# Routed layers of a decoder: indirect scatters into slots replaced by a list made on PE and indirect loads

## What is computed

```python
# L0f (top 2, GELU, hidden 512) and L2f (top 2, RMS norm, gated SiLU, hidden 448)
logits = h @ W_router                       # 2048 x 8
v, idx = top_k(logits, 2); w = softmax(v)
out = sum_k w[:, k] * expert[idx[:, k]](h)  # two products with W1, W2
# L1f (top 1, layer norm, GELU, hidden 512, at most 256 tokens of an expert)
p = softmax(logits); e = argmax(p)
out = p[e] * expert[e](h)  where the token's rank in its expert is below 256, else 0
```

## Time and profile before

| | us |
|---|---|
| median of 3 runs | 1659.69 (1654.34 to 1673.64) |
| the profiled execution | 1662.46 |
| its span | 1660.70 |
| PE busy in the span | 1188.7 (72%) |
| DVE busy | 1058.3 (64%) |
| ACT busy | 626.4 (38%) |
| POOL busy | 616.4 (37%) |

### The profile page before, as it was taken

One profiled execution on the slowest core, in us unless ns is written; L12 is line 12 of the kernel. 1 busy time (PEld: TensorE's weight loads), 2 busy tenths in 40 slices (PEclk: granted clock), 3 DMA queues, 4 the chain that ended last, 5 costly groups with the idle time before them and its releaser, 6 DMA issues. The chain is left out here.

```text
span 1660.7 us, 35597 instructions
## 1 busy us (share of the span) xinstructions
PE 1188.7 (72%) x14040; PEld 901.0 (54%) x14040; DVE 1058.3 (64%) x2869; ACT 626.4 (38%) x1475; POOL 616.4 (37%) x694
## 2 busy tenths in 40 slices
PE   6983508858999869664677854099938885776878
PEld 5652408746888646553344643088825551563556
DVE  4888711147999748835678498234379937856772
ACT  2551104314777736222454321022214433543433
POOL 4347353432333235443233025623343333424320
PEclk9995559978999879777687565599969866876879
DMA  8900035550000078031000100345410000000000
GB/s 267 153 3 2 12 100 162 185 168 23 3 3 3 3 100 110 6 91 55 1 1 1 27 1 9 105 132 182 150 51 2 1 1 1 2 2 1 1 1 26
DMA packets 72010, 89.13 MB, mean 54 GB/s; under 512 B 5823, under 2 KB 59138, under 8 KB 71200
## 3 DMA queue, kind: packets, MB, share of 16 engines
q1 hardware_dynamic: 65824, 76.89, 19.5%
q0 software_dynamic: 6016, 9.93, 1.7%
HBM read 56.55 MB, written 32.69 MB: 54 GB/s over the span
## 5 line engine op out<-in xcount | busy, mean ns | idle before, releaser
L766 POOL TENSOR_TENSOR arena<-arena,small 128x1024 f32<-128x1024 f32 x80 | 154.7, 1939 | 112.2 <-ACT arena L649 70.1
L380 POOL TENSOR_SCALAR var_eps<-moments 128x1 f32<-128x1 f32 (+1 forms) x136 | 35.7, 262 | 367.1 <-DVE moments L373 367.1
L697 ACT ACTIVATE arena<-arena 128x1024 f32<-128x1024 f32 x80 | 84.6, 1058 | 136.8 <-DVE arena L844 136.7
L564 PE MATMUL ps<-arena,q 64*64 64x512 f32 x640 | 103.3, 719 | 39.1 <-issue 17.6
L574 PEld LDWEIGHTS ps<-small,arena 128*128 128x128 f32 x640 | 82.7, 159 | 65.0 <-ACT arena L697 32.8
L722 ACT COPY arena<-ps 128x512 f32<-128x512 f32 x160 | 87.3, 588 | 67.3 <-PE ps L574 66.5
L574 PE MATMUL ps<-small,arena 128*128 128x128 f32 x640 | 100.4, 307 | 10.8 <-ACT arena L697 10.0
L1608 PEld LDWEIGHTS ps<-expert_ring,arena 128*128 128x128 f32 (+1 forms) x864 | 104.5, 192 | 2.9
L1608 PE MATMUL ps<-expert_ring,arena 128*128 128x128 f32 (+1 forms) x864 | 104.7, 275 | 0.0
L586 PE MATMUL ps<-vx,arena 128*64 128x18 f32 x2560 | 99.6, 222 | 3.1 <-issue 2.8
L586 PEld LDWEIGHTS ps<-vx,arena 128*64 128x64 f32 x2560 | 91.2, 151 | 18.4 <-issue 14.8
(11 more groups left out here) (360 smaller groups left out, 2925.6 us busy)
## 6 DMA issues: line engine op xcount, KB each, us to landing
expert_ring<-L2f_in SPq DMA_DIRECT2D x23, 704.0 KB, 4.2
expert_ring<-L0f_in SPq DMA_DIRECT2D x23, 578.0 KB
slots_L0f<-blank SPq DMA_DIRECT2D x1, 8385.0 KB, 56.7
slots_L2f<-blank SPq DMA_DIRECT2D x1, 8385.0 KB, 56.6
small<-small_in SPq DMA_DIRECT2D x1, 4231.5 KB, 19.2
expert_ring<-L1f_in SPq DMA_DIRECT2D x8, 512.0 KB
arena<-slots_L0f SPq DMA_DIRECT2D x23, 129.0 KB, 3.2
arena<-slots_L2f SPq DMA_DIRECT2D x23, 129.0 KB, 3.5
```

Of the source, the lines that this page charges most:

```text
L564: last = pe.matmul(c.ps[part(b), m], c.q[part(m), at:at + S], kx(t)[part(m), b * 512:(b + 1) * 512], start=True, stop=True)
L697: act.activation(buf(k), buf(k), ACT.Exp, scale=exp_scale).then_inc(s.probs_ready, 1)
L766: g.tensor_tensor(kx(t).rearrange("p (b h k) -> p b h k", b=2, k=S), bcast(of_tile, 2, HEADS // 2), bcast(bcast(c.w("head_of_row"), 2, S), ...
```

## The change

Rows no longer pass through a table of slots. SP stores the tokens plainly in DRAM, four DMAs as quarters become ready. For each quarter DVE (`mark_cells`) and POOL (`mark_columns`) form one-hot rows from the slot numbers: a slot is split into a column (its low seven bits) and a start, one operand holds the token's number + 1 at the start's place, the other a 1 at the column's. PE multiplies them and adds up over all tiles (`invert_slots`), which gives the number of the token in each slot. For top 2 a further product (`find_rows`) picks the rows of the 23 blocks; `list_rows` on DVE makes of them the tokens to fetch and the places to return to, and marks empty slots. POOL fetches each block with two indirect loads of 128 rows (`fetch`), four blocks ahead, in the same list as the returns. The blank tables, the row copies on ACT, the row loads of SP and the cast of `home` go; the blank table of L1f's results stays. Of the diff, cut:

```diff
@@ routed_experts: SP
-        sp.wait_ge(c.scattered, c.scattered_before[n] + 16 * NT * top)
-        for j in range(3):
-            load_rows(j, first[j])
-        for j in range(BLOCKS):
-            if j + 3 < BLOCKS:
-                load_rows(j + 3, row_of_block(j + 3))
-            if j >= SLOTS:
-                load_routed(j)
+        by_tile = tokens_dram.rearrange("(p t) d -> p t d", t=NT)
+        for q in range(QUARTERS):
+            if twice:
+                sp.wait_ge(r.ready, HT * (q + 1))
+            sp.dma_start(by_tile[:, own(q)], src[:, own(q)]).then_inc(s.stored, 16)
...
+        for j in range(SLOTS, BLOCKS):
+            load_routed(j)
@@ PE
+        def invert_slots(q):
+            pe.wait_ge(s.cells_a, HT * top * (q + 1))
+            pe.wait_ge(s.cells_b, HT * top * (q + 1))
+            for i in range(HT * top):
+                first, final = q == 0 and i == 0, q == QUARTERS - 1 and i == HT * top - 1
+                if capped:
+                    last = pe.matmul(found_ps, cells_b(q)[:, i], cells_a(q)[:, i], start=first, stop=final)
+                else:
+                    last = pe.matmul(inverse_ps, cells_a(q)[:, i], cells_b(q)[:, i], start=first, stop=final)
+            last.then_inc(s.inv_ps, 1)
+        def find_rows():
+            pe.wait_ge(s.inv_ready, 1)
+            pe.wait_ge(s.mapped, 11)
+            pe.matmul(found_ps, inverse, chosen, start=True, stop=True).then_inc(s.found_ps, 1)
...
             if q > 0:
                 rank(q - 1)
+            if q > 1:
+                invert_slots(q - 2)
...
+        invert_slots(QUARTERS - 2)
+        invert_slots(QUARTERS - 1)
+        if not capped:
+            find_rows()
@@ ACT
-            if not twice:
-                for k in range(top):
-                    act.copy(rows(k)[:, own(q), 0:D], c.h[:, own(q)]).then_inc(s.rows, 1)
-            if twice and top == 2:
-                act.wait_ge(r.ready, HT * (q + 1))
-                act.copy(rows(1)[:, own(q), 0:D], rows(0)[:, own(q), 0:D]).then_inc(s.rows, 1)
+        if not capped:
+            act.wait_ge(s.inv_ps, QUARTERS)
+            act.copy(inverse, inverse_ps).then_inc(s.inv_ready, 1)
@@ POOL
+        def mark_columns(q):
+            g.wait_ge(s.column, 3 * q + 2)
+            if q >= 2:
+                g.wait_ge(s.inv_ps, q - 1)
+            for i, t in enumerate(tiles_of(q)):
+                for k in range(top):
+                    g.tensor_scalar(cells_b(q)[:, i * top + k], c.w("lane"), T[:, t, 15, k:k + 1], None, ALU.is_equal)\
+                        .then_inc(s.cells_b, 1)
+        def fetch(j):
+            if j >= 5:
+                g.wait_ge(s.xT_ps, j - 4)
+            for k in range(PER):
+                at = c.token_of[:, PER * j + k:PER * j + k + 1]
+                g.indirect_dma_start(xs(j)[:, k], None, tokens_dram[:, :],
+                                     bass.IndirectOffsetOnAxis(ap=at, axis=0),
+                                     bounds_check=NT * P - 1, oob_is_err=False).then_inc(c.fetched[j % 5], 16)
         for q in range(QUARTERS):
-            g.wait_ge(s.slot_index, q + 1)
...
+            mark_columns(q)
+        g.wait_ge(s.stored, 16 * QUARTERS)
+        g.wait_ge(s.listed, 5)
+        for j in range(4):
+            fetch(j)
+        if capped:
+            g.wait_ge(c.blanked[n], 16)
         for j in range(BLOCKS):
+            if j + 4 < BLOCKS:
+                fetch(j + 4)
             g.wait_ge(s.y_ready, j + 1)
-            g.wait_ge(s.home, j + 1)
@@ DVE
-            v.tensor_scalar(c.slot[:, own(q), 0:top], T[:, own(q), 10, 0:top], float(NOWHERE) if capped else 0.0,
-                            None, ALU.add).then_inc(s.slot_index, 1)
+            v.tensor_scalar(slot, T[:, own(q), 10, 0:top], float(NOWHERE) if capped else 0.0, None, ALU.add)\
+                .then_inc(s.placed, 1)
+            v.wait_ge(s.placed, q + 1)
+            v.tensor_scalar(column, slot, P - 1, None, ALU.bitwise_and).then_inc(s.column, 1)
+            v.wait_ge(s.column, 3 * q + 1)
+            v.tensor_copy(T[:, own(q), 15, 0:top], column).then_inc(s.column, 1)
+            v.tensor_tensor(T[:, own(q), 15, 4:4 + top], slot, column, ALU.subtract).then_inc(s.column, 1)
+        def mark_cells(q):
+            v.wait_ge(s.column, 3 * q + 3)
...
+            for i, t in enumerate(tiles_of(q)):
+                for k in range(top):
+                    v.tensor_scalar(cells_a(q)[:, i * top + k], c.w("lane_start")[:, 0:CELLS], T[:, t, 15, 4 + k:5 + k],
+                                    numbers[:, k, t:t + 1], ALU.is_equal, ALU.mult).then_inc(s.cells_a, 1)
+        def list_rows():
...
+            v.tensor_scalar(number, found_ps, -1.0, 0.0, ALU.add, ALU.max).then_inc(s.listed, 1)
...
         place(0)
+        mark_cells(0)
...
         if not capped:
             map_blocks()
+        list_rows()
         weigh()
@@ take_slots: DVE
-            v.tensor_copy(c.home[:, PER * j:PER * j + PER], xs(j)[:, :, D]).then_inc(s.home, 1)
```

More of the change, by code:

```diff
@@ L292, in room, with blank_homes @@
         return self.arena[:, k * 1024:(k + n) * 1024]
[L294 to L297 removed]
+    def blank_homes(self, sp, n):
+        sp.dma_start(self.home_dram[n].rearrange("(p t) d -> p t d", t=NT), bcast(self.blank[:], 1, NT))\
             .then_inc(self.blanked[n], 16)
[L299 to L301 removed]
     def load_expert(self, sp, layer, e):
@@ L492, in attention @@
     block = c.block
[L493 to L496, removed]
     @block.tensor
@@ L1672, in _ @@
         for k in range(top):
-            g.tensor_scalar(rows(k)[:, :, D], c.w("token_home"), float(k * NT * P), None, ALU.add)\
+            g.tensor_scalar(numbers[:, k], c.w("token_number"), float(k * NT * P), None, ALU.add)\
                 .then_inc(s.constants, 1)
@@ L1766, in map_blocks @@
             count, upto_e = scratch(224, E), scratch(232, E)
-            of_block, region, before, inside, offset = (scratch(640 + 32 * k, TOP2_BLOCKS) for k in range(5))
+            of_block, region, before, inside, column = (scratch(640 + 32 * k, TOP2_BLOCKS) for k in range(5))
             by_j = lambda a: a.rearrange("p (j e) -> p j e", e=E)
@@ L1789, in map_blocks @@
             v.wait_ge(s.mapped, 9)
-            v.scalar_tensor_tensor(out=offset, in0=inside, scalar=float(PER * P), in1=region, op0=ALU.mult,
+            v.scalar_tensor_tensor(out=column, in0=inside, scalar=float(PER), in1=region, op0=ALU.mult,
                                    op1=ALU.add).then_inc(s.mapped, 1)
             v.wait_ge(s.mapped, 10)
-            v.tensor_scalar(c.block_row[:], offset[0:1], float(E * NT * P), None, ALU.min).then_inc(s.block_row, 1)
+            for k in range(PER):
+                last = v.tensor_scalar(chosen.rearrange("p (j k) -> p j k", k=PER)[:, :, k], column, float(k),
+                                       c.w("own_lane"), ALU.add, ALU.is_equal)
+            last.then_inc(s.mapped, 1)
         def weigh():
@@ L1864, in _ @@
         place(1)
+        mark_cells(1)
         for q in range(2, QUARTERS):
@@ L1867, in _ @@
             place(q)
+            mark_cells(q)
         if not capped:
             map_blocks()
+        list_rows()
         weigh()
@@ L1930, in _ @@
     def _(sp):
-        c.blank_slots(sp, "L1f")
+        c.blank_homes(sp, "L1f")
     @block.tensor
@@ L2774 @@
 STAGES = {
-    "L0a": lambda c: attention(c, "L0a", mode="bias", q_scale=HD ** -0.5, bias=True, out_bias=True,
-                               blanks="L0f"),
+    "L0a": lambda c: attention(c, "L0a", mode="bias", q_scale=HD ** -0.5, bias=True, out_bias=True),
     "L0x": channel_attention,
@@ L2779 @@
     "L1a": rotary_attention,
-    "L1x": lambda c: attention(c, "L1x", "ctx", exp_scale=HD ** -0.5, blanks="L2f"),
+    "L1x": lambda c: attention(c, "L1x", "ctx", exp_scale=HD ** -0.5),
     "L1f": lambda c: routed_experts(c, "L1f", 1, False),
@@ L2810, in decoder @@
         c.dram, c.context = big, context
-        c.slots_dram = {"L0f": nc.dram_tensor("slots_L0f", ((E * NT + 2) * P, D + 1), F32).ap(),
-                        "L1f": nc.dram_tensor("slots_L1f", (E * CAPACITY, D + 1), F32).ap(),
-                        "L2f": nc.dram_tensor("slots_L2f", ((E * NT + 2) * P, D + 1), F32).ap()}
+        c.tokens_dram = {n: nc.dram_tensor("tokens_" + n, (NT * P, D), F32).ap() for n in ("L0f", "L1f", "L2f")}
         c.home_dram = {n: nc.dram_tensor("home_" + n, (k * NT * P, D), F32).ap()
                        for n, k in (("L0f", 2), ("L1f", 1), ("L2f", 2))}
-        c.blanked = {n: ctx.enter_context(nc.semaphore(f"blanked_{n}")) for n in c.slots_dram}
-        c.scattered = ctx.enter_context(nc.semaphore("scattered"))
+        c.blanked = {"L1f": ctx.enter_context(nc.semaphore("blanked_L1f"))}
         c.returned = [ctx.enter_context(nc.semaphore(f"returned_{k}")) for k in range(4)]
-        c.scattered_before = {"L0f": 0, "L1f": 32 * NT, "L2f": 48 * NT}
         used = {"L0f": TOP2_BLOCKS, "L1f": E, "L2f": TOP2_BLOCKS}
```

(3 more changed lines are left out.)

100 lines of the change are left out of this document (51 added, 49 removed).

## The result

The changed kernel took 1683.98 us (median of 4 runs, 1675.77 to 1690.73), the kernel before 1661.29 us beside it (1654.34 to 1673.64): a ratio of 1.0147, 95% interval 1.0106 to 1.0189. It is slower by 23 us or 1.5%, and above the 1680 us at which the range of the prediction ended. The profiled execution took 1685.76 us (span 1683.9).

What follows compares the result with a forecast made beforehand. PE was taken to bound the loops, POOL the stretch ahead of each. L0f -3, L1f +6, L2f -11 gave -8, with 1 us a stage for marks -5.5: 1654 us against a median of 1659.69, range 1634 to 1680.

Steps and rivals of the forecast that it cites:

- Part 1: POOL's issues: 92, 32, 92 per stage, 0.97 us each, 5.11 us a block; POOL bounds L0f and L1f.
- e = 0.05: e is the extra us per fetch in the loops; the kernel was to be slower than before from e = 0.09.
- the fetches cost more: Rival, chance 0.2: dearer loop fetches on POOL; about 1678 us at 0.3 us more each, 1696 at 0.48.
- Part 2, the first fetch: L0f from logits to list: DVE quarters of 7.6 us, marks 3.2, PE's inversion 2.2; first fetch at 230.0 us.
- the list comes late: Rival, chance 0.18: POOL marks at 0.77 us each or DVE stalls as beside scatters; +8, about 1661 us.
- Part 2, from the first fetch to the first result: L0f: two issues, 1.2 us landing, then 9.5 us; first fetch at 230.0, first result at 242.9 us.
- The rule that I had set beside the row: Skill page's fixed part of about 2 us per transfer; each first block 0.8 us later, 2.4 in all.
- Parts 2 and 3, behind the last fetch: Two and a half PE blocks plus last returns; L0f then ends 3 us sooner, L1f 6 us later.
- Part 4: L2f: first result 11.4 us sooner, loop stays at PE's 5.46 us a block, end 11 us sooner.
- Part 3's meeting with the long addition: L1f: POOL's second issue meets weigh's 2.23 us addition on DVE and costs 1.4 us more.
- The 3 us for marks meeting DVE: 1 us added per routed stage for POOL's column marks running beside DVE's two-operand work.
- The clock rival: PE's clock falls to 1.2 GHz in L0f's paced loop: +42, about 1696 us; counted within dear fetches' chance 0.2.

Runs made afterwards that it cites:

- experiment 5: The changed kernel with six fetches ahead, PE waiting for each pair of marked tiles instead of the whole quarter's: 1658.71 us, ratio 0.9990.
- experiments 4: L2f as in the changed kernel, L0f and L1f as in the kernel before: 1660.85 us, ratio 1.0004 to the kernel before.
- 6: L1f as in the changed kernel, L0f and L2f as in the kernel before: 1668.40 us, ratio 1.0041 to the kernel before.
- experiment 7: The kernel before with the blank-row fills of L0f and L2f made twice: 1664.96 us, ratio 1.0005 to the kernel before.
- experiment 9: The kernel before with a fourth slot of expert weights: 1640.03 us, ratio 0.9868.
- 11: The kernel before with four weight slots and, in L2f alone, the list (six ahead, by product, up(0) earlier, split marks): 1640.00 us, ratio 0.9850.
- experiment 2: The changed kernel with up(0) ahead of turn_slots(1) in PE's order: 1677.24 us, ratio 1.0082 to the kernel before.
- experiment 12: The changed kernel with a fourth slot of expert weights and nothing else: 1674.86 us, ratio 1.0104 to the kernel before.

## Why the prediction was wrong

- **Part 1, POOL's count, was right in kind.** 92, 32 and 92 issues, a gapless queue, PE waiting for fetched rows, all as forecast. The term was mis-sized: an indirect load takes 1.00 to 1.04 us, not 0.97, and the returns among them up to 1.02: 1.325 us a piece instead of 1.28, 3.0 us over the 92 us (72 issues) that Part 2 had from the first return to the last fetch. That is e = 0.05, short of the 0.09 from which "the fetches cost more" would have made the kernel slower by itself; that rival is not what happened.
- **Part 2, the first fetch.** 2.4 us late in L0f, 1.4 and 1.1 in L1f and L2f. A mark on POOL costs 0.58 us, not 0.4 (inside the bounds), and the "eight 128x128 products, 2.2 us" are sixteen instructions and 3.5 us. The sum had them one behind the other, as the trace shows them, so what failed is the two prices: 1.6 and 1.3 us in L0f, of which short steps behind them gave 0.5 back. Waiting product by product (experiment 5) takes 1.3 to 2.3 us off. DVE's quarter of 7.6 us was right (7.4 to 7.8), so the rival "the list comes late" was true in its sign and too small to decide. Its other half, that DVE stalls as it does "beside scatters", and the stall that Part 2 saw in map_blocks, rest on one profile: experiments 4, 6, 7, 9 and 11 issue the same scatters in L0f and have no stall there.
- **Part 2, from the first fetch to the first result.** 2.4, 3.0 and 3.0 us too short. The landing of 1.2 us came from return scatters at the end of L0f, where little else moves. The first block's rows were there 1.7 us after its last issue in L0f, 2.9 in L1f and 1.8 in L2f, and in the loops a fetch takes 3.3 us from its issue, 2.3 beyond the instruction. And in PE's order turn_slots(1) stands ahead of up(0), so the first result hangs on the second block too, which POOL now issues 2.6 us later instead of SP at once; experiment 2 gives 0.6 to 1.3 us of it back.
- The rule that I had set beside the row and left out of the sum was nearer to the truth here: the fetches show 1.7 to 2.9. The Trainium skill, "DMA: Bandwidth & Descriptors", section "Anatomy of one DMA — SWDGE (gpsimd) path", gives the fixed part as about 2 us, and the trace agrees in size.
- **Parts 2 and 3, behind the last fetch.** "Two and a half blocks of PE and the last returns" were 15.0 us in L0f and 13.8 in L1f; they took 16.9 and 18.7. In L1f PE stood idle 3.14 us for the last rows, and then its first products ran at the lower level (3.58 us at 767.30 for what took 1.89 at 772.50), granted 0.86 between 760 and 772 us. Here the fetch distance was the real fault: with six ahead the end of L1f comes 7.3 us sooner with the same number of issues, at a granted clock of 1.00 to its end. I had taken "four blocks ahead" as given.
- **Part 4, "the loop stays at PE's 5.46", is the largest single step that failed**: 7.2 us. I compared PE with POOL and left out the third stream. The expert loads had been just in time, at 4.2 us from issue to landing; with 46 fetches beside them they take 4.7, three slots leave no room, and PE was busy 93% of this loop and not over 95%. A fourth slot alone brings the loop back to 119.3 us (experiment 12). POOL was closer too than the sum had it: 5.30 us a block beside PE's 5.46, where 5.11 had left 7 us of slack over the loop; but with four slots it still fits. Of the loads I had only said that they wait on the same results. I had written that they were "close behind in L0f" and drawn nothing from it; the row is PE's 9.4 us of waits for expert_ring, shown under experiment 9.
- **Part 3's meeting with the long addition** came as predicted, once a stage, at half the price: the fetch beside it took 1.80 us in L1f and 1.81 in L2f instead of 1.0, 0.8 us and not 1.4. The stretched row of 2.45 us had met more of the addition: it began 0.61 us after it, the fetches 1.30 and 1.35, and all three ended 0.8 to 0.9 us after its end. The 3 us for marks meeting DVE were shown by no row and show nowhere by themselves; the even 0.58 us of a mark includes them if there are any.
- **The clock rival** did not come true. In L0f's paced loop the granted clock was 0.98, and where it was 0.91 (experiment 12) the loop was as long.
- **Edits at nothing**: the fills are shown (experiment 7). The stores and ACT's copies were not tried by themselves.

By terms, predicted against measured: first fetch 2.4 + 1.4 + 1.1, fetch to return 2.4 + 3.0 + 3.0, POOL's period 3.0 + 0.2, behind the last fetch 1.9 + 4.9, L2f's loop 7.2, together 30.5 us (rounded terms apart); -9.1 + 30.5 = 21.4, the 21.4 of the table. This is the bookkeeping of one profile each, with the 3 us of luck in each of L0f and L2f on the side of the kernel before.

## What to carry over

When transfers are moved onto a queue that also carries the results, count its issues per turn and then choose the fetch distance anew: here the same issues cost 17 us less over three stages with six blocks ahead than with four. A loop has as many bounds as it has streams, so ask of each of them (weights too) how long it takes from issue to landing and when it is issued, not how busy it is; the rows of waits name the one that is just in time, and a ring with one more slot may be worth more than the change at hand, as it was here.

## What I had not expected of the hardware

- The fetches slow L2f's loads of weights (704 KB) though the DMA engines are little more than half busy (share 0.54 in L2f's loop, 0.50 before). From issue to landing they take 4.2 us in the changed kernel without the loops' fetches and 4.0 to 4.3 in the kernels with scatters; with fetches in the loop the medians are 4.4 to 5.3, with no order between three slots and four. L0f's loads (578 KB) take 3.7 to 4.0 with or without.
- The first indirect load of a stage holds POOL 1.30 us in L0f and 1.18 or 1.19 in L1f and L2f, in every run, and the ones behind it 1.00.
- What two profiles of the same code can differ by within a stage: 3 us from the last scatter to the first load of rows (5.5 and 5.6 us in L0f and L2f of the kernel before, 2.4 to 2.6 in five other profiles with the same scatters), and idle times of up to 3.3 us ahead of short DVE instructions of the routing that none of the five has. A wait that one profile shows need not be the kernel's; a second profile of it is worth its price before a sum is built on it. The cause stays open.
